# Keys and queries of the first two batches in a row ahead of the loop, and loads in another order, in a cross-attention and expert layer

## The chip, the cores and the metric

One core of one Trainium2 chip runs the whole layer. The metric is the device time of one execution in microseconds; lower is better. TensorE (PE) multiplies, VectorE (DVE), ScalarE (ACT) and GpSimd (POOL) do the elementwise work, and SyncE (SP) issues most of the DMA transfers. Each engine runs its own instructions strictly in the order in which they are written, and waits on semaphores for the others.

## The reference

Eight batches; x is 112 x 256 for each, the context 375 x 256, and attention has 16 heads of 16.

```python
q = split_heads(layernorm(x) @ Wq + bq); k = split_heads(ctx @ Wk + bk); v = split_heads(ctx @ Wv + bv)
scores = where(mask, -1e15, q @ k.T / sqrt(16))
x = x + tanh(g_xattn) * (softmax(scores) @ v @ Wo + bo)
h = layernorm(x)                      # then, for each batch, the three likeliest of 8 zones:
w = top3(softmax(tanh(mean(h) @ W1 + b1) @ W2 + b2)), normalised
x = x + tanh(g_ffn) * (h + sum_e w_e * gelu(h @ Wa[e]) @ Wb[e])
```

## The kernel before

The program has an attention stage, which is a software pipeline over the batches, and then an expert stage of 24 units (8 batches, 3 zones each). Its instructions are written out by hand for each engine.

**The pipeline.** The loop `for b in range(-2, B)` on every engine has a body for each b from -2 to 7, and each body four slots. Body b works on several batches at once: it turns batch b's scores into exponentials and sums (`st_tile`, `exp_tile`, `pv`), makes the row maxima of batch n = b + 1 (`s1` on TensorE, `row_max` on VectorE), the values of n (`V0`, `V1`), the keys and queries of batch m = b + 2 (`CX0`, `CX1`, `XT`, `K0`, `K1`, `Q`), and finishes batch o = b - 1. A step for a batch that isn't there is left out, so body -2 holds only the keys and queries of batch 0, and body -1 those of batch 1 together with row maxima and values of batch 0. The first exponential of the program is `exp_tile(0, 0, 0)`, at the head of body 0 on ScalarE.

**Keys and queries.** Context and normalised x are transposed (L1057, L1083) and copied to SBUF, K and Q are projected (L1066, L1092), ScalarE rounds them to float16 (`k_hi` L645, `q_hi` L637) and VectorE makes the remainder (`k_lo` L811, `q_lo` L819). SyncE writes both to a scratch in HBM (`write_k` L316, `write_q` L310) and, when the write has landed, reads them back in another layout (`read_k` L339, four issues for each half of the heads; `read_q` L327, two). `s1` (L1016) of a batch waits for both.

**The scratch buffers.** `k_hl`, `q_hl`, `ctx_s`, `xa`, `mask_s` and `tT` exist once. A batch's K and Q therefore wait until those of the batch before have been written, and a load into them until the batch before has been read.

**The expert weights.** While the attention runs, the weights of all 8 zones stream in through a ring (`stage`) in 64 parts, two in a slot, from slot 2 of body -1 on. One load of 512 KB brings two parts (`load_parts`, L359 and L362, on SyncE, two slots ahead of use). GpSimd scales a part (`scale_part`, L459), ScalarE rounds it (`w_hi`, L655), GpSimd makes the remainder (`lo_part`, L464). GpSimd's order in a slot is: scale the two parts of the next slot, then the norm or the bias step of this slot, then the remainders of this slot's two parts. In slot 3 of body b the norm is `norm1(b + 3)` (L469, L470). ScalarE's order at the end of a body is `v_copy` (L605), `w_hi` of the slot's two parts, `normed` (L586), which waits for that norm. `tanh_gates` (L611, L615) comes after it in body -2.

**SyncE's order in a body** is: `read_k` and `read_q` of the second half of n, `move_max(b, 1)`, parts, the loads of context and x of batch m + 1, the mask of m, parts, the writes of m, `move_max(n, 0)` (L348; `st_tile` of a batch waits for it), parts, the reads of the first half of m, parts.

**PSUM.** The small steps share three banks in turn (`MISC_BANKS`); `Spare` lists their order, and TensorE waits in `use` until the bank's last user is done.

Of the kernel before, what the change touches and what calls it, by code (L numbers as in the profile page):

```python
# [14 lines left out]
B, SQ, D, SK = 8, 112, 256, 375  # L15
# [45 lines left out]

def slot_uses(b, slot):

    n, m, o = b + 1, b + 2, b - 1
    every = (
        (("MX1", b), ("CX0", m), ("CX1", m), ("XT", m), ("OT", o), ("K0", m)),
        (("K1", m), ("Q", m), ("X2T", b - 2)),
        (("MX0", n), ("V0", n), ("ON", o)),
        (("V1", n), ("OP", o)),
    )  # L70
    more = {(B - 2, 3): ("H", 0), (B - 1, 0): ("L", 0), (B - 1, 2): ("W", 0), (-1, 3): ("BO", 0)}.get((b, slot))
    return [u for u in every[slot] if there(u[1])] + ([more] if more else [])


TAIL = {0: ("OT", B - 1), 1: ("X2T", B - 2), 2: ("ON", B - 1), 3: ("OP", B - 1), 5: ("X2T", B - 1), 7: ("H", 1), 8: ("L", 1), 11: ("W", 1)}
# [12 lines left out]
class Spare:  # L88


    def __init__(self):
        names, banks = [], []
        for b in range(-2, B):
            for slot in range(4):
                for name in slot_uses(b, slot):
                    banks.append(MISC_BANKS[len(names) % len(MISC_BANKS)])
                    names.append(name)
        for i, name in enumerate(TAIL.values()):
            names.append(name)
            banks.append(TAIL_BANKS[i % len(TAIL_BANKS)])  # L100
        self.at = {name: i for i, name in enumerate(names)}
        self.names, self.banks = names, banks
# [38 lines left out]
def flamingo_layer(nc, x, ctx, mask, g_xattn, g_ffn, Wq, bq, Wk, bk, Wv, bv, Wo, bo,  # L141
                   W1, b1, W2, b2, Wa, Wb, out):
    with ExitStack() as stack:
# [124 lines left out]
        def view_w(ap):  # L268
            return ap.rearrange("(t p) n -> p t n", p=128)
# [17 lines left out]
        def _(sp):  # L287
# [111 lines left out]
            load_ctx(0)  # L399
            sp.dma_start(wqkvo[:, 2, :, :], view_w(Wv)).then_inc(s["wv_loaded"], 16)  # L400
            for b in range(-2, B):
                n, m, o = b + 1, b + 2, b - 1
                read_k(n, 1)
                read_q(n, 1)
                move_max(b, 1)
                load_parts(b, 0)
                load_xr(o)
                load_ctx(m + 1)
                load_x(m + 1)
                load_mask(m)  # L410
                load_parts(b, 1)
                write_k(m, 0)
                write_k(m, 1)
                write_q(m)
                move_max(n, 0)
                load_parts(b, 2)
                if b == B - 1:
                    store_index(0)
                    sp.wait_ge(s["xt_done"], B)
                    load_r(0)  # L420
                    sp.wait_ge(s["misc_full"], spare.full(("V1", B - 1)))
                    load_x2(0)
                    load_x2(1)

                read_k(m, 0)
                read_q(m, 0)
                load_parts(b, 3)
                store_r(b - 2)
                store_x2(b - 2)
# [21 lines left out]
        def _(pool):  # L451
# [46 lines left out]
            pool.wait_ge(s["zeroed"], 5)  # L498
# [3 lines left out]
            g.dma_start(bo_r[:, :], bass.AP(bo.tensor, 0, [[0, 128], [1, D]])).then_inc(s["const_loaded"], 16)  # L502
            g.dma_start(w1_s[:, :, :], W1.rearrange("(t p) n -> p t n", p=128)).then_inc(s["const_loaded"], 16)
            g.dma_start(w2_s[:, :], W2).then_inc(s["const_loaded"], 16)
            g.dma_start(b1_c[:, :], b1.rearrange("(p o) -> p o", o=1), allow_slow_non_contiguous=True).then_inc(s["const_loaded"], 16)
            g.dma_start(b2_r[:, :], bass.AP(b2.tensor, 0, [[0, B], [1, NZ]])).then_inc(s["const_loaded"], 16)
            for b in range(-2, B):
                for slot in range(4):
# [9 lines left out]
                    for k in ks:  # L518
                        lo_part(k)
            norm2(B - 2)  # L520
# [4 lines left out]
        def _(act):  # L525
            a = nc.scalar
            a.dma_start(wq_in, view_w(Wq)).then_inc(s["wq_loaded"], 16)
            a.dma_start(wqkvo[:, 1, :, :], view_w(Wk)).then_inc(s["wk_loaded"], 16)
            a.dma_start(bk_c[:, :], bk.rearrange("(t p) -> p t", p=128), allow_slow_non_contiguous=True).then_inc(s["bk_loaded"], 16)
            for t in range(DT):  # L530
                a.dma_start(bq_c[:, t:t + 1], bass.AP(bq.tensor, t * 128, [[1, HD], [HD, PAIRS], [1, 1]]), allow_slow_non_contiguous=True).then_inc(s["bq_loaded"], 16)
            a.dma_start(bv_c[:, :], bv.rearrange("(t p) -> p t", p=128), allow_slow_non_contiguous=True).then_inc(s["bv_loaded"], 16)
            a.dma_start(gates[:, 0:1], bass.AP(g_xattn.tensor, 0, [[0, 128], [1, 1]])).then_inc(s["g_loaded"], 16)
            a.dma_start(gates[:, 1:2], bass.AP(g_ffn.tensor, 0, [[0, 128], [1, 1]])).then_inc(s["g_loaded"], 16)
            a.dma_start(wqkvo[:, 3, :, :], view_w(Wo)).then_inc(s["wo_loaded"], 16)
# [38 lines left out]
            def mask_bias(b):  # L574
                if there(b):
# [3 lines left out]
                    if b == 0:  # L579
                        act.wait_ge(s["zeroed"], 5)  # L580
# [88 lines left out]
            normed(0)  # L669
            act.wait_ge(s["wq_loaded"], 16)  # L670
            a.activation(wq_p[:, :, :, :], wq_in.rearrange("p k (t j i) -> p (k t) i j", t=DT, i=HD), ACT.Copy, scale=HD ** -0.5).then_inc(s["wq_scaled"], 1)
            for b in range(-2, B):
                n, m, o = b + 1, b + 2, b - 1
# [7 lines left out]
                if b == -2:  # L681
                    act.wait_ge(s["bq_loaded"], 32)
                    a.activation(bq_c[:, :], bq_c[:, :], ACT.Copy, scale=HD ** -0.5).then_inc(s["wq_scaled"], 1)
                    act.wait_ge(s["wq_scaled"], 2)
                    act.wait_ge(s["bk_loaded"], 16)
# [32 lines left out]
                normed(m + 1)  # L718
                if b == -2:
                    tanh_gates()  # L720
# [36 lines left out]
        def _(dve):  # L757
# [139 lines left out]
            v.memset(qbd[:].rearrange("p a e j f -> p (a e j f)"), 0.0).then_inc(s["zeroed"], 1)  # L897
            v.memset(vp[:].rearrange("p a c h i -> p (a c h i)"), 1.0).then_inc(s["zeroed"], 1)
            v.memset(bank[:, O_BANK, :], 0.0).then_inc(s["zeroed"], 1)
            ln1_stats(0)  # L900
            v.memset(maskb[96:KQ, :, :], 1.0).then_inc(s["zeroed"], 1)
            v.memset(pT[96:CK + 1, :, :], 1.0).then_inc(s["zeroed"], 1)
            dve.wait_ge(s["zeroed"], 5)
            for b in range(-2, B):
                n, m, o = b + 1, b + 2, b - 1
# [8 lines left out]
                if b == -2:  # L914
                    dve.wait_ge(s["wq_scaled"], 2)
                    dve.wait_ge(s["bk_loaded"], 16)
# [12 lines left out]
                ln1_stats(m + 1)  # L929
# [12 lines left out]
                if b == -1:  # L942
# [52 lines left out]
        def _(pe):  # L995
# [41 lines left out]
            def pv(b, g):  # L1037

                if there(b):
                    pe.wait_ge(s["act_exp"], tile(b, g, 2) + 1)  # L1040
                    if g == 0:
                        pe.wait_ge(s["v_done"], 2 * b + 2)
                        need(pe, s["act_o"], b)
# [137 lines left out]
            pe.wait_ge(s["zeroed"], 3)  # L1181
            for b in range(-2, B):
# [102 lines left out]
```

## Time and profile before

| | |
|---|---|
| time, median of 3 runs (lowest to highest) | 330.56 us (330.47 to 331.02) |
| the profiled execution: its own time / its span | 328.42 us / 326.3 us |
| mean granted TensorE clock | 0.984 of full |
| busy: PE, DVE, ACT, POOL | 289.3, 203.2, 195.5, 134.3 us |
| DMA | 40.51 MB, mean 124 GB/s |

The span is the time from the first to the last instruction of the profiled execution, and times inside it count from its start. Its own time is 2.1 us longer than the span. Sums are made against 328.42 us and then set against the median. "Landing" is the moment at which a transfer's semaphore is complete.

### The profile page before, as it was taken

What the parts mean: (1) busy time and instruction counts of PE and PEld (TensorE: products, weight loads), DVE (VectorE), ACT (ScalarE), POOL (GpSimd) and SP (SyncE); (2) the same over time, 40 slices, a digit from 0 to 9 for tenths busy, and PEclk for the clock granted to TensorE, in tenths of its full rate; (3) what the DMA queues carried; (4) which work ended last, traced back from release to release, by engine and by line L of the source; (5) the groups of instructions that cost most, each with busy time, mean ns of one, the idle gap of its engine ahead of it and who ended that gap; (6) DMA issues with size and microseconds to landing.
All of it is one profiled execution on the core that took longest, in us unless ns stands there. A gap on an engine that the chain in (4) does not pass through costs nothing.

```text
span 326.3 us, 9360 instructions
## 1 busy us (share of the span) xinstructions
PE 289.3 (89%) x3348; PEld 242.0 (74%) x3348; DVE 203.2 (62%) x617; ACT 195.5 (60%) x406; POOL 134.3 (41%) x185
## 2 busy tenths in 40 slices
PE   1619679899989999999989867999999999999996
PEld 1406457676766766767666646999999999999996
DVE  7417838576787777877687545656564745636542
ACT  2413466877878778777787876635454753543531
POOL 3401576867778689687788871000000000000000
PEclk9978979999999999999999999999999999999999
DMA  7458776787677977868664512101110110101000
GB/s 163 123 152 234 177 226 161 214 250 182 196 206 176 274 211 191 255 182 242 180 191 145 147 44 58 33 27 33 41 33 2 44 31 17 44 2 44 2 16 14
DMA packets 39324, 40.51 MB, mean 124 GB/s; under 512 B 10249, under 2 KB 35137, under 8 KB 39281
## 3 DMA queue, kind: packets, MB, share of 16 engines
q1 hardware_dynamic: 37168, 38.94, 42.7%
q10 hardware_dynamic: 1936, 0.79, 1.0%
q8 instruction: 28, 0.46, 0.6%
q0 software_dynamic: 176, 0.20, 0.3%
q14 instruction: 16, 0.12, 0.1%
HBM read 33.09 MB, written 6.74 MB: 122 GB/s over the span
## 4 chain that ended last, share of the span: by engine, by line
PE 64%; DMA 9%; ACT 7%; DVE 5%; issue 5%; SPq 5%; POOL 2%; ACTq 0%; DVEq 0%
PE bank L1240 18%; PE bank L1221 16%; PE bank L1066 6%; PE bank L1075 4%; PE bank L1016 4%; DMA qbd<-q_scr 4%; PE bank L1028 4%; PE bank L1032 3%; PE bank L1048 3%; ACT pT L545 2%; DMA stage<-in_L_ffn_Wa 2%; PE bank L1057 2%; SPq L339 2%; PE bank L1132 2%; ACT wa L655 2%
## 5 line engine op out<-in xcount | busy, mean ns | idle before, releaser
L769 DVE CUSTOM_DVE_ANT_0 bank<-bank,maskb 112x375 f32<-112x375 f32 x128 | 67.9, 571 | 39.8 <-PE bank L1016 39.7
L1240 PE MATMUL bank<-wb,stage 128*112 x576 | 66.8, 273 | 0.0
L1240 PEld LDWEIGHTS bank<-wb,stage 128*112 128x112 f16 x576 | 62.2, 130 | 0.2
L1221 PE MATMUL bank<-ctxT,wqkvo 128*128 128x112 f16 x960 | 59.4, 213 | 2.0 <-DVE qbd L895 1.3
L1221 PEld LDWEIGHTS bank<-ctxT,wqkvo 128*128 128x128 f16 x960 | 57.5, 98 | 2.9 <-issue 2.2
L732 ACT ACTIVATE kst<-bank 128x448 f32<-128x448 f32 x48 | 25.6, 534 | 55.4 <-PE bank L1221 55.3
L545 ACT ACTIVATE pT<-bank 125x448 f32<-125x448 f32 x96 | 48.9, 539 | 9.0 <-PE bank L1032 8.3
L894 DVE COPY wqkvo<-wa 128x3072 f16 x24 | 23.2, 969 | 48.5 <-PE bank L1221 47.5
L459 POOL TENSOR_SCALAR stage<-stage 128x512 f32<-128x512 f32 x64 | 38.5, 618 | 26.5 <-DMA stage<-in_L_ffn_Wa 21.7
L1016 PE MATMUL bank<-kst,qbd 128*112 128x375 f16 x128 | 33.8, 338 | 15.2 <-DMA qbd<-q_scr 11.8
L464 POOL TENSOR_TENSOR wb<-stage,wb 128x512 f16<-128x512 f32 x32 | 37.5, 1191 | 14.0 <-ACT wb L655 14.0
L1028 PE MATMUL bank<-rq,maskb 115*128 115x448 bf16 (+1 forms) x96 | 35.5, 370 | 7.5 <-ACT pT L545 7.1
L1221 PE MATMUL bank<-ctxT,qbd 128*128 128x112 f16 x192 | 40.9, 213 | 0.0
L464 POOL TENSOR_TENSOR wa<-stage,wa 128x512 f16<-128x512 f32 x32 | 36.4, 1159 | 10.0 <-ACT wa L655 10.0
L1032 PE MATMUL bank<-qbd,kst 128*128 128x224 f16 (+1 forms) x192 | 34.4, 260 | 0.0
L958 DVE SCALAR_TENSOR_TENSOR stage<-kst,wbc,stage 128x448 f16<-128x448 f32 x48 | 30.9, 680 | 3.9 <-ACT stage L734 3.8
L734 ACT ACTIVATE stage<-kst,wbc 128x448 f16<-128x448 f32 x48 | 32.1, 669 | 1.6
L1032 PEld LDWEIGHTS bank<-qbd,kst 128*128 128x128 f16 (+1 forms) x192 | 21.6, 113 | 11.7 <-issue 1.3
L1016 PEld LDWEIGHTS bank<-kst,qbd 128*112 128x112 f16 x128 | 15.0, 132 | 19.9 <-DMA qbd<-q_scr 12.8
L1048 PE MATMUL bank<-pT,vp 125*17 125x112 f32 (+1 forms) x768 | 24.7, 261 | 0.0
L469 POOL TENSOR_TENSOR rstd<-ve,half 112x1 f32<-112x1 f32 x16 | 8.8, 551 | 37.0 <-DVE ve L791 37.0
L1028 PEld LDWEIGHTS bank<-rq,maskb 115*128 115x128 bf16 (+1 forms) x96 | 10.7, 111 | 14.9 <-ACT pT L545 12.7
(123 smaller groups left out, 423.6 us busy)
## 6 DMA issues: line engine op xcount, KB each, us to landing
stage<-in_L_ffn_Wa SPq DMA_DIRECT2D x16, 512.0 KB, 4.3
stage<-in_L_ffn_Wb SPq DMA_DIRECT2D x16, 512.0 KB, 4.4
kst<-k_scr SPq DMA_DIRECT2D x64, 93.8 KB, 3.7
k_scr<-wb SPq DMA_DIRECT2D x16, 187.5 KB
ctx_s<-in_ctx SPq DMA_DIRECT2D x8, 336.0 KB
qbd<-q_scr SPq DMA_DIRECT2D x32, 56.0 KB, 3.1
xa<-in_x SPq DMA_DIRECT2D x8, 112.0 KB, 4.4
q_scr<-wb SPq DMA_DIRECT2D x16, 56.0 KB, 3.2
```

The costliest lines, as they stand in the source:

```text
L459: g.tensor_scalar(st, st, WSCALE, 1.0, ALU.mult, ALU.mult).then_inc(s["scaled"], 1)
L464: g.tensor_tensor(part_dst(k, 1), stage[:, k % RING, :], part_dst(k, 0), ALU.subtract).then_inc(s["lo_done"], 1)
L545: a.activation(pT[0:CK, t % PRING, :], bank[0:CK, ST_BANKS[t % len(ST_BANKS)], 0:QUAD], ACT.Exp).then_inc(s["act_exp"], 1)
L734: a.activation(hT[:, u % 2, cols], h_w[:, cols], ACT.Copy, scale=wbc[:, u:u + 1]).then_inc(s["hthi_done"], 1)
L769: v.tensor_tensor_reduce(out=bank[0:SQ, e, 0:SK], in0=bank[0:SQ, e, 0:SK], in1=maskb[0:SQ, b % 2, 0:SK], scale=-1.0, scalar=FLOOR, op0=ALU ...
L958: v.scalar_tensor_tensor(out=hT[:, u % 2, (2 + hf) * QUAD:(3 + hf) * QUAD], in0=h_w[:, cols], scalar=wbc[:, u:u + 1], in1=hT[:, u % 2, col ...
L1016: T.matmul(bank[0:SQ, e, 0:SK], qbd[:, b % 2, e, p, :], kst[:, b % 2, p * SK:(p + 1) * SK], start=True, stop=True).then_inc(s["pe_s1"], 1)
L1028: T.matmul(o[0:w, :].rearrange("k (j q) -> k j q", j=4), maskb[0:KQ, b % 2, c * CK:c * CK + w], rq[0:KQ, g // 2, :, g % 2, :], start=True, ...
L1032: ins = T.matmul(o[0:w, i * 2 * SQ:(i + 1) * 2 * SQ].rearrange("k (e q) -> k e q", e=2), kst[:, b % 2, p * SK + c * CK:p * SK + c * CK + w ...
L1048: ins = T.matmul(bank[32 * j:32 * j + VC, O_BANK, g * SQ:(g + 1) * SQ], vp[0:k, b % 2, c, h, :], pT[0:k, tile(b, g, c) % PRING, j * SQ:(j ...
L1221: ins = T.matmul(o, first(ws, t, f), x2b[:, b % 2, (xs * DT + t) * SQ:(xs * DT + t + 1) * SQ], start=(t == 0 and xs == 0 and ws == 0), sto ...
L1240: ins = T.matmul(o, hT[:, u % 2, hs * FT * SQ + f * SQ:hs * FT * SQ + (f + 1) * SQ], wb[:, bass.ds(e * (4 * CHUNK) + ws * (2 * CHUNK) + f ...
```

## The change

The keys and queries of batches 0 and 1 are made in a row ahead of the loop (`AHEAD`), and the loop starts with body -1. `made(b)` gives b + 2 from body 0 on and nothing in body -1, which now holds only the row maxima and the values of batch 0. The loads change places: Wk goes before Wq on ScalarE's queue; bk, bq, Wv, Wo, bv and the two gates go to SyncE's queue, the last four into body -1; GpSimd's five loads of constants go to the end of body -1. `tanh_gates` goes to the end of body -1, and the constant term of the output bias (`BO`, L1102) to body 0. The memsets of VectorE are spread between its first steps, and TensorE no longer waits for three of them.

```diff
+def made(b):
+    return b + 2 if b >= 0 else B
-    more = {..., (-1, 3): ("BO", 0)}.get((b, slot))
+    more = {..., (0, 3): ("BO", 0)}.get((b, slot))
+AHEAD = (("CX0", 0), ("CX1", 0), ("XT", 0), ("K0", 0), ("K1", 0), ("Q", 0),
+         ("CX0", 1), ("CX1", 1), ("K0", 1), ("K1", 1), ("XT", 1), ("Q", 1))
@@ SyncE
             load_x(0)
             load_ctx(0)
+            sp.dma_start(bk_c ...)
+            for t in range(DT): sp.dma_start(bq_c ...)
+            load_mask(0)
+            load_ctx(1)
+            load_x(1)
+            write_k(0, 0)
+            write_k(0, 1)
+            write_q(0)
+            for h in range(2):
+                read_k(0, h)
+                read_q(0, h)
             sp.dma_start(wqkvo[:, 2, :, :], view_w(Wv))
-            for b in range(-2, B):
-                n, m, o = b + 1, b + 2, b - 1
-                read_k(n, 1)
-                read_q(n, 1)
+            load_mask(1)
+            write_k(1, 0)
+            write_k(1, 1)
+            write_q(1)
+            for h in range(2):
+                read_k(1, h)
+                read_q(1, h)
+            for b in range(-1, B):
+                n, m, o = b + 1, made(b), b - 1
+                if n > 1:
+                    read_k(n, 1)
+                    read_q(n, 1)
                 move_max(b, 1)
                 load_parts(b, 0)
                 load_xr(o)
-                load_ctx(m + 1)
-                load_x(m + 1)
+                load_ctx(b + 3)
+                load_x(b + 3)
                 load_mask(m)
+                if b == -1: Wo, bv and the two gates are loaded here
                 load_parts(b, 1)
@@ GpSimd
+            norm1(1)
-            pool.wait_ge(s["zeroed"], 5)
+            pool.wait_ge(s["zeroed"], 4)
...
-            g.dma_start(bo_r ...), w1_s, w2_s, b1_c, b2_r
-            for b in range(-2, B):
+            for b in range(-1, B):
...
                     for k in ks:
                         lo_part(k)
+                    if (b, slot) == (-1, 3): the five loads of bo_r, w1_s, w2_s, b1_c, b2_r
@@ ScalarE
+            a.dma_start(wqkvo[:, 1, :, :], view_w(Wk))
             a.dma_start(wq_in, view_w(Wq))
-            the loads of Wk, bk_c, bq_c, bv_c, gates, Wo
...
             normed(0)
+            cx_copy(0)
+            xt_copy(0)
             (Wq and bq scaled)
+            k_hi(0, 0); k_hi(0, 1); q_hi(0)
+            cx_copy(1); mask_bias(0); normed(1)
+            k_hi(1, 0); k_hi(1, 1); xt_copy(1); q_hi(1); mask_bias(1)
-            for b in range(-2, B):
+            for b in range(-1, B):
...
-                normed(m + 1)
-                if b == -2:
+                normed(b + 3)
+                if b == -1:
                     tanh_gates()
@@ VectorE
             v.memset(qbd)
-            v.memset(vp); v.memset(bank)
             ln1_stats(0)
+            v.memset(bank); v.memset(maskb)
+            cx_copy(0); k_lo(0, 0); k_lo(0, 1); q_lo(0)
+            ln1_stats(1)
+            cx_copy(1)
+            v.memset(vp)
+            k_lo(1, 0); k_lo(1, 1)
             v.memset(pT)
+            q_lo(1)
-            for b in range(-2, B):
+            for b in range(-1, B):
...
-                ln1_stats(m + 1)
+                ln1_stats(b + 3)
@@ TensorE
-            pe.wait_ge(s["zeroed"], 3)
-            for b in range(-2, B):
+            for name in AHEAD:
+                put(name)
+            for b in range(-1, B):
```

## Rows read from the trace of the kernel before

**Rows 1.** The profile page, part 4: the chain that ended last, by engine.

```profile
PE 64%; DMA 9%; ACT 7%; DVE 5%; issue 5%; SPq 5%; POOL 2%; ACTq 0%; DVEq 0%
```

**Rows 2.** Stretches: length, busy us (instructions) by engine, granted clock, DMA share, GB/s.

```profile
23.60:42.40 18.80, 13.90 (x61) 9.41 (x61) 13.45 (x52) 6.91 (x16) 6.91 (x11) 0.92 0.73 198
42.40:62.96 20.56, 18.99 (x165) 13.83 (x165) 13.17 (x50) 14.56 (x33) 13.77 (x17) 0.92 0.69 196
62.96:83.10 20.14, 19.34 (x199) 14.60 (x200) 13.77 (x53) 15.57 (x36) 15.14 (x20) 1.00 0.76 213
```

**Rows 3.** Timeline, start: start, length, engine, line, what, [idle before <-releaser].

```profile
6.80 1.48 PE L1057 MATMUL bank<-ident,ctx_s 125*128 125x125 f32 x6 [6.80 <-DVE maskb L901]
...
7.21 1.93 DVE L902 MEMSET pT<- 30x2240 f32 x1 [0.42 <-issue]
...
9.98 4.25 PE L1066 MATMUL bank<-ctxT,wqkvo 128*128 128x375 f32 x8 [1.32 <-DVE ctxT L805]
...
12.94 0.57 ACT L645 ACTIVATE wb<-bank,bk_c 128x375 f16<-128x375 f32 x1 [3.55 <-PE bank L1066]
...
14.87 0.61 DVE L811 SCALAR_TENSOR_TENSOR wb<-bank,bk_c,wb 128x375 f16<-128x375 f32 x1 [0.59 <-ACT wb L645]
```

**Rows 4.** Timeline: the issues of SyncE's queue around its first reads.

```profile
14.30 1.80 SPq L316 DMA_DIRECT2D k_scr<-wb  x2
...
18.34 2.23 SPq L339 DMA_DIRECT2D kst<-k_scr  x4
...
21.93 1.97 SPq L339 DMA_DIRECT2D kst<-k_scr  x4
...
23.94 1.16 SPq L327 DMA_DIRECT2D qbd<-q_scr  x2
...
25.14 0.59 SPq L359 DMA_DIRECT2D stage<-in_L_ffn_Wa  x1
...
26.37 0.83 SPq L299 DMA_DIRECT2D ctx_s<-in_ctx  x2
...
28.10 0.43 SPq L359 DMA_DIRECT2D stage<-in_L_ffn_Wa  x1
```

**Rows 5.** Timeline: first and last of four issues on ScalarE's queue.

```profile
3.59 0.61 ACTq L532 DMA_DIRECT2D bv_c<-in_L_xattn_bv  x1
...
5.22 0.46 ACTq L535 DMA_DIRECT2D wqkvo<-in_L_xattn_Wo  x1
```

**Rows 6.** Writes of k_scr, whole run: issue to landing.

```profile
DMA to landing us min/median/max: 1.9/3.7/4.2
```

**Rows 7.** Loads of stage, whole run: issue to landing.

```profile
DMA to landing us min/median/max: 3.6/4.4/6.2
```

**Rows 8.** Timeline: GpSimd and ScalarE before the first exponential.

```profile
18.95 0.72 ACT L615 ACTIVATE wqkvo<-wqkvo,tgate 128x512 f32<-128x512 f32 x1
...
30.05 1.20 POOL L459 TENSOR_SCALAR stage<-stage 128x512 f32<-128x512 f32 x2 [11.86 <-DMA stage<-in_L_ffn_Wa]
...
37.81 2.27 POOL L464 TENSOR_TENSOR wa<-stage,wa 128x512 f16<-128x512 f32 x2 [3.60 <-ACT wa L655]
...
41.22 0.54 POOL L469 TENSOR_TENSOR rstd<-ve,half 112x1 f32<-112x1 f32 x1
...
42.07 0.60 ACT L586 ACTIVATE xa<-xa,nmr,rstd 112x256 f32<-112x256 f32 x1 [1.43 <-POOL nmr L470]
...
42.57 0.52 ACT L545 ACTIVATE pT<-bank 125x448 f32<-125x448 f32 x1
```

**Rows 9.** Timeline: TensorE at the start of body 0.

```profile
42.45 0.53 PE L1016 MATMUL bank<-kst,qbd 128*112 128x375 f16 x2 [2.11 <-DMA qbd<-q_scr]
...
44.64 0.58 PE L1028 MATMUL bank<-rq,maskb 115*125 115x448 bf16 x1
```

**Rows 10.** Timeline: last of five issues by GpSimd.

```profile
12.43 0.56 POOL L506 DMA_DIRECT2D b_r<-in_L_ffn_b  x1
```

## The prediction on record

> **What bounds the kernel now.** I read the chain that ended last first, because it says which engines the end hangs on [rows 1]. TensorE holds 64% of it; DMA, SyncE's queue and ScalarE hold another 21%. Next I cut the span at the moments at which TensorE opens a body [rows 2]. Body -1 (23.6 to 42.4) has TensorE busy 13.90 of 18.8 us, body 0 has 18.99 of 20.56, body 1 has 19.34 of 20.14. From body 0 on the attention stage is TensorE's, with almost nothing idle. A delay ahead of body 0 therefore reaches the end, and so does a gain. What counts is one moment: when body 0 can really run. I call it by `exp_tile(0, 0, 0)`, which starts at 42.57 [rows 8]. TensorE's third scores tile needs that exponential.
>
> Before 42.57 two chains arrive nearly together, and that is the point of this profile. One is the round trip of batch 1's keys and queries: TensorE waits 2.11 us for them until 42.45 [rows 9]. The other is the expert weights on GpSimd and ScalarE: remainders of parts 0 and 1 from 37.81, scaling of the next two, the norm of batch 2 at 41.22, `normed(2)` at 42.07, then the exponential [rows 8]. ScalarE and GpSimd take their work in written order, so this second chain holds the exponential as firmly as the first. The change shortens the first chain. I ask what it does to the second.
>
> **The start.** Before, VectorE's copy of the context waited behind a memset that began at 7.21 and took 1.93; K began at 9.98, its first half reached ScalarE at 12.94, and the last remainder of K ended at 14.87 + 0.61 [rows 3]. The memset goes behind the copy. The transposes, from 6.80 for 1.48, end at 8.28; a copy and the hand-over take some 0.8, so K starts at about 9.1: a gain of 0.8 to 1.1 (the context may land a little earlier, as Wv is not behind it). The eight records of K took 4.25 us, the first half of them 2.96 and the second 1.3: the first half ran at half pace. With a shorter pause of TensorE ahead of K more of it could run at the full pace, up to 1.3 more. I take a gain of 1.5 in all, with 0.8 and 2.4 as ends. The shorter memset order, the order of Wk and Wq, and TensorE's dropped wait have no price of their own beyond this: the copies they stood before are in it. The Trainium skill (TensorE: Matmul & The Clock Gate, "What's actually happening") says that the half pace ends after sustained activity; by that the gain here would be 2.4 and the total 0.9 us lower. No row before shows TensorE working through from the transposes, so I don't rest on it.
>
> **SyncE's queue, the step that decides.** Before, it ended batch 0's reads at 23.94 + 1.16 = 25.10, and issued the first load of parts at 25.14, context and x of batch 2 from 26.37, the second load of parts at 28.10; batch 1's writes and reads came only after those [rows 4]. In the change all of batch 1's round trip stands before the first load of parts:
> - reads of batch 0 end at 25.10 - 1.5 = 23.6;
> - Wv and mask 1, two issues like those of parts and context, 0.45 each: 24.5;
> - two writes of K, 0.65 each, the second issued at 25.15, and two of Q at 0.55: 26.9;
> - the second write of K lands 3.7 later [rows 6], at 28.85. SyncE waits for it with `read_k` half issued. The remaining two issues take it to 29.8, `read_q` 1.25 to 31.05, the second halves 2.0 and 1.2 [rows 4] to 34.25;
> - the first load of parts is issued at 34.25 instead of 25.14, and until 34.85;
> - two issues of context and one of x: 26.37 to 28.10 held four issues with the mask [rows 4], so 1.3: 36.15;
> - Wo, bv and two gates, which took 3.59 to 5.68 on ScalarE's queue [rows 5], 2.1: 38.25;
> - the second load of parts is issued at 38.25 instead of 28.10.
>
> The Trainium skill (DMA: Bandwidth & Descriptors, "Issuing engines are not separate DMA queues") says that a second issuing engine saves only issue time. The rows agree that this time is what counts: the four issues moved cost 2.1 us of SyncE.
>
> **From the second load to the exponential.** It lands 4.8 after its issue (the first took 4.9 to its use [rows 4, 8]; all loads 3.6 to 6.2 [rows 7]): 43.05. GpSimd then does, in its written order, two scalings 1.20, the remainders of parts 0 and 1 2.27, two scalings 1.20, and the norm 0.81 (41.22 to 42.03, by the start of what it released) [rows 8]: 48.55. The remainders can't go ahead of the scaling that waits. ScalarE does `normed(2)` 0.6 and then the moved `tanh_gates`, 0.72 and a tanh of 0.2 [rows 8]: 50.1. The exponential starts at about 50.1 instead of 42.57, 7.5 us later.
>
> **What of it reaches TensorE.** Before, TensorE's third tile began at 44.64 [rows 9], 2.07 after the exponential's start, since the late queries had also held `s1(1, 0)`. In the change `s1(1, 0)`, the second tile and the context's transposes are done while it waits, and the third tile can follow 0.6 after: 1.45 comes back. VectorE has its own wait: x of batch 2 is issued at 35.8 and lands about 40, `ln1_stats(2)` stands ahead of the last four row maxima of batch 0, and those end near 44. TensorE's V1, first tiles and transposes then end near 48.3, under cover of the 50.1; without that cover it would cost 1 to 2 us. What is queued behind ScalarE's wait is everything of body 0. `BO` moves into body 0, which TensorE fills: four passes, at most the 1.3 of half a K [rows 3], against 1.6 us idle in that body [rows 2]. I take 0.3, ends 0 and 0.9.
>
> GpSimd's five loads of constants, at 0.6 each about 3.1 (the last took 0.56 [rows 10]), now stand between remainders 2, 3 and the scaling of parts 6, 7. ScalarE wants those parts only after batch 2's queries, several microseconds on. That hides them; the load of parts 10, with `write_k(2, 0)` behind it on SyncE, goes 1 to 2 us late, but `write_k(2, 1)` is later still and sets the read. Without cover they cost up to 3.1. Batch 1's second reads leave body 0 (3.1 us of SyncE), which had nothing waiting on them.
>
> **The sum.** 7.5 - 1.45 + 0.3 = 6.4 us on 328.42, so 334.8 by the profiled execution, which stands 2.14 under the median of the runs. Against 330.56 the forecast is 337.0. For the low end: a start gain of 2.4 (-0.9), reads that never wait for a write (-1.25), parts that land in 3.6 (-1.2): 333.6, or 333.3 without `BO`. For the high end: start gain 0.8 (+0.7), writes at 4.2 (+0.5), parts at 6.2 (+1.4), `BO` at 0.9 (+0.6): 340.2.
>
> **The rivals.**
> - *Faster, because the second chain isn't the one that ends last.* The row ahead overlaps batch 1's projections with batch 0's round trip; batch 1's operands land near 34 instead of 42.4. For it speaks the 2.11 us wait [rows 9]. Then body 0 would open with the move of the maxima at about 41.5, and with the 1.45 the time would be about 328.5. It decides only if the second load of parts is issued before about 31.9 (38.25 less 6.4), and twelve read issues of 6 us stand before it. The Trainium skill (DMA: Bandwidth & Descriptors, "Rules for kernel authors") advises to issue early and wait late, which this change does for the keys and undoes for the parts. 6%.
> - *The delay is won back.* The chain holds 9% DMA and 5% SyncE [rows 1], part of it accidents of phase in later bodies, such as a load of parts that took 6.2 [rows 7]. If one or two don't recur, 3 us come back: 333.9. Against it: bodies 0 and 1 are nearly full [rows 2]. 13%.
> - *A second hold.* GpSimd's constants lose their cover, and parts and writes in body 0 go late by 3.1: 340.1, more with a slow landing. 12%.
> - *Nothing moves*, all gains and holds cancelling: 330.6. 3%.
>
> **Numbers.** The forecast has 66%, its own range 334 to 340. The range to hold 8 in 10 takes in the low and most of the high end: 333.3 to 340.2. Within 0.2% is what a measurement of this kernel can't tell from no change. Slower 91%, same 3%, faster 6%.
>
> **What would show it.** K from about 9 instead of 9.98; the loads of parts at about 34 and 38; GpSimd idle for them and `norm1(2)` near 48; ScalarE waiting for it ahead of an exponential near 50; TensorE idle some ten microseconds within batch 0's row maxima, and body 0's stretch no shorter. The prediction is wrong if the loads of parts are issued before 32, if SyncE finds batch 1's writes landed and its issues much shorter, or if bodies 1 to 6 become shorter than before.

## The result, and the profile after

The changed kernel takes 340.22 us, median of 4 runs (339.82 to 345.49), against 330.79 us for the kernel before in the same runs; the ratio is 1.0272, with a 95% interval of 1.0202 to 1.0342. It is 9.4 us slower. Medians are of all runs; a ratio leaves out single runs that took over 1.5% longer than the fastest of their kernel, so it need not be the quotient of the two medians. The forecast was slower by 6.4, at 337.0, within 333.3 to 340.2. The direction and the chain were right; the size was short by a third, and the time lies on the upper edge of the range, just outside the 334 to 340 that the forecast itself was given.

The profiled execution took 339.82 us, with a span of 337.6 against 326.3. That is 11.3 us more, not 9.4: the kernel before scatters from 327.9 to 334.0 over the 23 runs beside the last experiments, and its profiled execution (328.42) was one of its quick ones. The sum was made on the profiled execution. There the upper end of the range is 338.1 (340.2 less 2.14), and 339.82 is 1.8 above it. That the median still touches the range is luck of this scatter.

The chain that ended last now has less TensorE and more DMA, SyncE and GpSimd than in [rows 1]:

```profile
PE 59%; DMA 13%; SPq 8%; ACT 6%; POOL 6%; issue 5%; DVE 2%; ACTq 0%; DVEq 0%
```

The stretches of the changed kernel, in the columns of [rows 2]: the row maxima of batch 0 until body 0 is ready to start, the wait until TensorE's third scores tile, and the rest of body 0.

```profile
23.10:47.10 24.00, 11.46 (x30) 6.14 (x31) 12.48 (x46) 3.06 (x7) 1.21 (x2) 0.59 0.67 181
47.10:54.80 7.70, 2.94 (x19) 1.72 (x17) 1.99 (x8) 3.47 (x8) 7.27 (x10) 0.93 0.30 102
54.80:73.90 19.10, 18.30 (x156) 13.14 (x157) 11.93 (x46) 13.73 (x31) 15.49 (x22) 0.91 0.67 177
```

TensorE is busy half of the first stretch and 2.94 of 7.70 us of the second, in which GpSimd is busy 7.27: GpSimd is the holder, TensorE the held. In body 0 TensorE is full, as it was.

The start, timeline, against [rows 3]:

```profile
6.56 1.48 PE L1107 MATMUL bank<-ident,ctx_s 125*128 125x125 f32 x6 [6.56 <-DMA ctx_s<-in_ctx]
...
8.89 5.28 PE L1116 MATMUL bank<-ctxT,wqkvo 128*128 128x375 f32 x8 [0.47 <-DVE ctxT L845]
...
14.81 0.61 DVE L851 SCALAR_TENSOR_TENSOR wb<-bank,bk_c,wb 128x375 f16<-128x375 f32 x1 [1.63 <-ACT wb L673]
```

K starts 1.09 us sooner, as forecast (0.8 to 1.1). But all its eight records now ran at half pace, 5.28 us against 4.25, and the last remainder ends at 15.42 against 15.48: nothing is gained.

SyncE's queue, timeline, against [rows 4, 5]:

```profile
23.58 1.15 SPq L335 DMA_DIRECT2D qbd<-q_scr  x2
...
25.92 1.28 SPq L324 DMA_DIRECT2D k_scr<-wb  x2
...
27.25 1.97 SPq L318 DMA_DIRECT2D q_scr<-wb  x2
...
30.00 2.46 SPq L347 DMA_DIRECT2D kst<-k_scr  x4
...
35.76 1.15 SPq L335 DMA_DIRECT2D qbd<-q_scr  x2
...
36.96 0.59 SPq L367 DMA_DIRECT2D stage<-in_L_ffn_Wa  x1
...
38.95 0.43 SPq L440 DMA_DIRECT2D wqkvo<-in_L_xattn_Wo  x1
...
40.91 0.43 SPq L367 DMA_DIRECT2D stage<-in_L_ffn_Wa  x1
```

The two loads of parts go out at 36.96 and 40.91; before, 25.14 and 28.10.

GpSimd, ScalarE, VectorE and TensorE ahead of the first exponential, timeline, against [rows 8, 9, 10]:

```profile
41.61 1.21 POOL L492 TENSOR_SCALAR stage<-stage 128x512 f32<-128x512 f32 x2 [21.84 <-DMA stage<-in_L_ffn_Wa]
...
43.34 0.43 DVE L828 BATCH_NORM_STATS2 stat<-xa 112x6 f32<-112x256 f32 x1 [10.41 <-DMA xa<-in_x]
...
44.94 1.07 PE L1064 MATMUL bank<-kst,qbd 128*112 128x375 f16 x2 [9.47 <-DVE peaks L809]
...
47.45 1.20 POOL L492 TENSOR_SCALAR stage<-stage 128x512 f32<-128x512 f32 x2 [4.63 <-DMA stage<-in_L_ffn_Wa]
...
48.61 2.27 POOL L497 TENSOR_TENSOR wa<-stage,wa 128x512 f16<-128x512 f32 x2
...
52.01 0.55 POOL L502 TENSOR_TENSOR rstd<-ve,half 112x1 f32<-112x1 f32 x1
...
52.86 0.60 ACT L614 ACTIVATE xa<-xa,nmr,rstd 112x256 f32<-112x256 f32 x1 [3.55 <-POOL nmr L503]
...
54.21 0.96 ACT L573 ACTIVATE pT<-bank 125x448 f32<-125x448 f32 x2
...
54.79 0.53 PE L1076 MATMUL bank<-rq,maskb 115*125 115x448 bf16 x1 [4.75 <-ACT pT L573]
...
54.98 0.81 POOL L550 DMA_DIRECT2D bo_r<-in_L_xattn_bo  x1
```

This is the chain as it was forecast, step for step: GpSimd waits for the second load (4.63), scales, makes remainders, scales, norms; ScalarE waits 3.55 for the norm; TensorE waits 4.75 for the exponential. GpSimd's loads of constants (54.98) come right behind. The longest wait of TensorE is another one, its 9.47 us in batch 0's row maxima, behind VectorE's 10.41 us for x of batch 2. Whether that one costs anything is the first question to the experiments. The first exponential came at 54.21 (forecast 50.1), TensorE's third tile at 54.79.

### The profile page after: what moved, and what is told of

The parts are those of the page before. It is cut to its first block, busy times and chain, and to the rows that moved or that the text cites. A ratio compares the mean times of both kernels' runs of the same rounds, so it can differ in the third digit from the quotient of the medians.

```text
span 337.6 us, 9361 instructions
## 1 busy us (share of the span) xinstructions
PE 295.1 (87%) x3348; PEld 242.9 (72%) x3348; DVE 203.0 (60%) x617; ACT 195.7 (58%) x406; POOL 134.1 (40%) x185
## 3 DMA queue, kind: packets, MB, share of 16 engines
q1 hardware_dynamic: 38560, 39.21, 42.5%
## 4 chain that ended last, share of the span: by engine, by line
PE 59%; DMA 13%; SPq 8%; ACT 6%; POOL 6%; issue 5%; DVE 2%; ACTq 0%; DVEq 0%
PE bank L1291 17%; PE bank L1272 16%; PE bank L1116 6%; DMA stage<-in_L_ffn_Wa 3%; PE bank L1125 3%; PE bank L1076 3%; DMA stage<-in_L_ffn_Wb 3%; PE bank L1064 3%; SPq L347 3%; DMA k_scr<-wb 3%; PE bank L1080 2%; PE bank L1098 2%; POOL stage L492 2%; SPq L335 2%; POOL wa L497 2%
## 5 line engine op out<-in xcount | busy, mean ns | idle before, releaser
L1064 PE MATMUL bank<-kst,qbd 128*112 128x375 f16 x128 | 35.4, 351 | 13.6 <-DVE peaks L809 12.1
L497 POOL TENSOR_TENSOR wb<-stage,wb 128x512 f16<-128x512 f32 x32 | 37.6, 1195 | 11.5 <-ACT wb L683 11.5
```

What stands on the lines that cost most here:

```text
L497: g.tensor_tensor(part_dst(k, 1), stage[:, k % RING, :], part_dst(k, 0), ALU.subtract).then_inc(s["lo_done"], 1)
L1064: T.matmul(bank[0:SQ, e, 0:SK], qbd[:, b % 2, e, p, :], kst[:, b % 2, p * SK:(p + 1) * SK], start=True, stop=True).then_inc(s["pe_s1"], 1)
```

## The experiments

Twelve kernels. Each row below is read from its profiled execution: the first exponential, TensorE's third scores tile, and the first residual step of VectorE (end of body 1), which shows what has come through to the steady part of the loop. The last column is the median of its runs, the others are single executions, which scatter by some us in their later parts; the kernel before had 330.75, 331.03 and 331.04 beside the three groups (1 to 4, 5 to 8, 9 to 12).

| | first exponential | third tile | first residual | time |
|---|---|---|---|---|
| before | 42.57 | 44.64 | 82.88 | 330.8 |
| changed | 54.21 | 54.79 | 93.69 | 340.22 |
| 1 two loads of parts first | 49.84 | 50.42 | 90.03 | 336.28 |
| 2 x of batch 2 first | 54.16 | 54.74 | 93.43 | 340.20 |
| 3 three loads and x first | 46.64 | 49.46 | 87.25 | 332.29 |
| 4 before, parts late | 50.67 | 51.25 | 89.84 | 338.90 |
| 5 gates back | 49.82 | 50.40 | 92.09 | 340.16 |
| 6 constants back | 53.09 | 53.67 | 93.41 | 340.93 |
| 7 TensorE kept at work | 52.72 | 53.30 | 92.77 | 340.59 |
| 8 all moved | 44.47 | 46.36 | 83.80 | 331.61 |
| 9 gates and constants back | 50.68 | 51.26 | 88.56 | 333.53 |
| 10 all moved, reordered | 39.97 | 45.06 | 83.22 | 330.54 |
| 11 norm earlier | 50.28 | 50.86 | 94.51 | 341.57 |
| 12 before, TensorE kept at work | 45.99 | 46.57 | 83.81 | 328.55 |

**1. The first two loads of parts ahead of batch 1's reads.**

```diff
             write_q(1)
+            load_parts(-1, 0)
+            load_parts(-1, 1)
             for h in range(2):
                 read_k(1, h)
                 read_q(1, h)
```

(Here and in 2, 3, 8 and 10 the calls in the loop for what is moved are skipped in body -1.)

> The changed kernel, with the first two loads of parts issued ahead of batch 1's reads. Theory (the late loads of parts hold GpSimd, and its norm of batch 2 holds the first exponential): the second load lands near 35 instead of 47.4, the next hold is the third load, still behind everything (issued near 42, landed near 46.5), so the norm comes near 48 and the first exponential near 50 instead of 54.2; time about 4 us below the changed kernel, 336. Rival (x of batch 2, for which VectorE and TensorE wait some 10 us, is what costs): it stays late, so no gain, 340.

336.28 us, ratio to before 1.0174 (1.0127 to 1.0221); first exponential at 49.84. The third load was used at 46.48 and the norm came at 47.64, both within 0.4 of the theory; only the second load came 1.2 later than expected (36.17). x of batch 2 stayed late (42.57), so the rival is out.

**2. x of batch 2 alone ahead of batch 1's reads.**

```diff
             write_q(1)
+            load_x(2)
             for h in range(2):
```

> The changed kernel, with x of batch 2 alone issued ahead of batch 1's reads. Theory: TensorE's pause of 9.5 us in batch 0's row maxima goes, the first exponential stays near 54, the time stays at 340 within 0.5. Rival (x of batch 2 costs): the time falls by 5 us or more, to 335 or less.

340.20 us. The timeline of this kernel, VectorE's statistics, TensorE's first scores tile, and the exponential with the third tile:

```profile
32.67 0.43 DVE L830 BATCH_NORM_STATS2 stat<-xa 112x6 f32<-112x256 f32 x1 [0.25 <-DMA xa<-in_x]
...
46.48 0.56 PE L1078 MATMUL bank<-rq,maskb 115*128 115x448 bf16 x1 [9.33 <-DMA rq<-ms]
...
54.16 0.96 ACT L575 ACTIVATE pT<-bank 125x448 f32<-125x448 f32 x2
54.74 0.63 PE L1078 MATMUL bank<-rq,maskb 115*125 115x448 bf16 x1 [4.24 <-ACT pT L575]
```

VectorE's wait is gone, x was used at 32.67 instead of 43.34, and the exponential did not move by 0.1 us. TensorE's pause did not go, as the theory had it: the row maxima are done sooner, and TensorE then stands 9.33 us before its first scores tile for the move of the maxima, which SyncE issues at 40.56 behind the first two loads of parts, context 2 and the gates. That tile comes at 46.48, 1.0 sooner than in the changed kernel, and still 7.7 before the exponential. So late x of batch 2 cost nothing, because another chain ended later. The move of the maxima is a third chain, with no price as long as GpSimd's is the last.

**3. Three loads of parts and x of batch 2 ahead of batch 1's reads.**

```diff
             write_q(1)
+            load_parts(-1, 0)
+            load_parts(-1, 1)
+            load_parts(-1, 2)
+            load_x(2)
             for h in range(2):
```

> The changed kernel, with the first three loads of parts and x of batch 2 all ahead of batch 1's reads. Theory: the GpSimd chain is done near 41; the move of the maxima (landed near 44) and the gates' loads (landed near 44) hold next, the first exponential comes near 45.3; time about 8.5 us below the changed kernel, 331.5, near the kernel before. Rival (VectorE's wait alone costs): as the run with x alone. Rival (the row of keys and queries itself costs, whatever the loads do): stays above 336.

332.29 us, ratio 1.0036 (1.0003 to 1.0069). First exponential at 46.64, 1.3 later than expected. Of the 9.4 us, 7.9 come back with the row of keys and queries left exactly as it is. So the row is not what costs; its place in front of the loads is. What holds the exponential now is the third chain: TensorE's first tile waits for the move of the maxima until 45.64, and ScalarE's tanh for the gates until 45.78. In the kernel before that tile came at 39.79.

**4. The kernel before, with only its first three loads of parts behind the first half of batch 1's reads.**

```diff
-                load_parts(b, 0)
+                if b != -1:
+                    load_parts(b, 0)
...
                 read_q(m, 0)
+                if b == -1:
+                    for i in range(3):
+                        load_parts(b, i)
```

(The calls for slots 1 and 2 are guarded in the same way.)

> The kernel before, with nothing of the row: only its first three loads of parts are issued after the first half of batch 1's reads. Theory: the loads go out near 39 instead of 25 to 35, the norm of batch 2 comes near 50 and the first exponential near 51 instead of 42.6; TensorE gets 1.5 back; time 7 us above the kernel before, 337.5. Rival (the row is what costs): within 1 us of the kernel before, since its keys and queries come as before.

338.90 us, ratio 1.0272 (1.0209 to 1.0334). This is the opposite test: nothing of the row, only the late loads, and the kernel before becomes slower by 8.15 us, where the changed one is slower by 9.4. Its timeline, SyncE, GpSimd, ScalarE:

```profile
39.07 1.06 SPq L359 DMA_DIRECT2D stage<-in_L_ffn_Wa  x2
...
49.32 0.54 POOL L475 TENSOR_TENSOR rstd<-ve,half 112x1 f32<-112x1 f32 x1
...
50.16 0.60 ACT L592 ACTIVATE xa<-xa,nmr,rstd 112x256 f32<-112x256 f32 x1 [3.00 <-POOL nmr L476]
50.67 0.96 ACT L551 ACTIVATE pT<-bank 125x448 f32<-125x448 f32 x2
```

**5. Wo, bv and the gates back on ScalarE's queue, the tanh ahead of the loop.**

```diff
             a.dma_start(wq_in, view_w(Wq))
+            a.dma_start(wqkvo[:, 3, :, :], view_w(Wo)).then_inc(s["wo_loaded"], 16)
...
             mask_bias(1)
+            tanh_gates()
```

(With it the loads of bv and the two gates; the four loads on SyncE and the later tanh are taken out.)

> The changed kernel, with Wo, bv and the two gates back on ScalarE's queue at the start, and the tanh of the gates ahead of the loop. Theory: SyncE issues the second load of parts 2 us sooner and ScalarE has 0.8 us less between the norm and the first exponential: 2.8 us below the changed kernel, 337.4. Rival (those issues are hidden): no difference.

340.16 us, no difference in time, although the first exponential came 4.4 us sooner. The gain was there at the third tile (50.40), mostly gone at the first residual (92.09 against 93.69), and wholly at the last one of the attention stage (209.18 against 209.04).

**6. GpSimd's five loads of constants back ahead of its loop.**

```diff
+            g.dma_start(bo_r[:, :], bass.AP(bo.tensor, 0, [[0, 128], [1, D]])).then_inc(s["const_loaded"], 16)
...
             for b in range(-1, B):
```

(With it the four other loads; the five at the end of body -1 are taken out.)

> The changed kernel, with GpSimd's five loads of constants back ahead of its loop. Theory (they are covered in body 0): within 0.5 us of the changed kernel. Rival (a second hold): 1 to 3 us below it.

340.93 us, 0.7 above the changed kernel and so within the scatter of its runs (338.96 to 341.92): covered, as the theory says.

**7. TensorE kept at work until the first context is there.**

```diff
             pe.wait_ge(s["ident_ready"], 1)
+            for i in range(11):
+                T.matmul(bank[:, ST_BANKS[0], 0:128], ident[:, :], ident[:, :], start=True, stop=True)
             for name in AHEAD:
```

> The changed kernel, with eleven extra products of the identity on TensorE (their result is not used) while it waits for the first context, 1.7 to 6.4 us. In the changed kernel all eight passes of batch 0's K ran at half pace, 5.28 us. Theory A (TensorE must have worked without a long pause before it gets its full pace): K takes about 2.7 us, batch 0's round trip ends 2 us sooner, everything behind it as well: 338. Theory B (the pace comes with time from the start, whatever TensorE does): K stays at 5.3 us and the time at 340.

340.59 us. Its timeline, TensorE at the start:

```profile
1.68 5.00 PE L1232 MATMUL bank<-ident 128*128 128x128 f32 x22 [1.68 <-POOL ident L521]
...
8.24 2.76 PE L1116 MATMUL bank<-ctxT,wqkvo 128*128 128x375 f32 x8 [0.66 <-DVE ctxT L845]
```

K in 2.76 us instead of 5.28, and the second load of parts issued at 39.38 instead of 40.91: theory A on the pace. The first exponential followed by 1.5, the first residual by 0.9, and the median not at all. So the pace was as theory A has it, and the time was as theory B has it.

**8. All of these moves together** (experiments 3, 5 and 6, and context 2 with the move of the maxima between the halves of batch 1's reads).

```diff
             write_q(1)
+            load_parts(-1, 0)
+            load_parts(-1, 1)
+            load_parts(-1, 2)
+            load_x(2)
             for h in range(2):
                 read_k(1, h)
                 read_q(1, h)
+                if h == 0:
+                    load_ctx(2)
+                    move_max(0, 0)
```

> The changed kernel's row, with the first three loads of parts and x of batch 2 ahead of batch 1's reads, context 2 and the first move of the maxima between their halves, the gates, bv and Wo back on ScalarE's queue with an early tanh, and GpSimd's constants ahead of its loop. Theory: nothing is left in front of the norm of batch 2 but two landed loads; the first exponential comes near 41.5, TensorE's third tile near 42.3 instead of 44.6: 328.5, about 2 us below the kernel before. Rival (the row costs in itself, by half-pace work of TensorE or by crowding of the transfers): 331 or more.

331.61 us, ratio 0.9997 (0.9948 to 1.0046): the same as the kernel before, not 2 us better. The first exponential came at 44.47, 3 us later than expected. x of batch 2 was issued at 30.15, right behind three loads of 512 KB, and used at 38.16; the move of the maxima, 5 KB issued at 35.36, was used at 42.86. Both engines were waiting for them when they came (5.77 and 0.33 us). These two small transfers, behind large ones on one queue, took 7 to 8 us. The rival's "crowding" is what the trace shows.

**9. Experiments 5 and 6 together.**

> The changed kernel with both parts moved back at once: Wo, bv, the gates and their tanh, and GpSimd's five loads of constants. Alone, the first brought the first exponential forward by 4.4 us and the second by 1.1, and neither brought the time below the changed kernel's. Theory (second hold: with the gates back, GpSimd's five issues, 3.1 us, stand before the remainders on which the load of parts 10 and the write of K behind it wait): the first exponential near 49, the write of batch 2's K waits for nothing but VectorE; 336.5, 3.5 us below the changed kernel. Rival (the gain is lost in later bodies, to TensorE's half pace): 339 to 341.

333.53 us, ratio 1.0108 (1.0051 to 1.0165). Two edits that did nothing alone save 6.7 us together (340.22 less 333.53), more than the 3.5 expected. Against experiment 5 the first residual is 3.5 sooner and the last one of the attention stage 6.2 (202.99 against 209.18), so nearly half of the gain comes in later bodies, where it was not followed. How the first part comes about is seen with experiment 11.

**11. Only GpSimd's norm of batch 2 moved, from slot 3 to slot 2 of body -1.**

```diff
                 for slot in range(4):
                     ks = parts_at(b, slot)
+                    if (b, slot) == (-1, 2):
+                        norm1(b + 3)
                     for k in parts_at(b + (slot + 1) // 4, (slot + 1) % 4):
                         scale_part(k)
...
-                    if slot == 3:
+                    if slot == 3 and b > -1:
                         norm1(b + 3)
```

> The changed kernel with one thing moved, no load and no transfer: GpSimd's norm of batch 2 is done in slot 2 ahead of the scaling of parts 2 and 3, not in slot 3 behind four scalings and two remainders. Theory (GpSimd's written order holds the first exponential): ScalarE's wait moves from the norm to the second load of parts (47.4); the first exponential comes at 50.7 instead of 54.2; time 3 us below the changed kernel, 337. Rival (the exponential is held by something else): no difference.

The exponential at 50.28 for 50.7 expected: no load moved, and the move of the norm in GpSimd's written order alone gave 3.9 us. That shows the first hold. But the time is 341.57, no better than the changed kernel's. The timeline of experiment 11, GpSimd and SyncE, then TensorE at batch 2's first row maxima:

```profile
47.17 1.20 POOL L492 TENSOR_SCALAR stage<-stage 128x512 f32<-128x512 f32 x2 [2.35 <-DMA stage<-in_L_ffn_Wa]
...
51.74 2.28 POOL L497 TENSOR_TENSOR wa<-stage,wa 128x512 f16<-128x512 f32 x2
...
53.95 0.81 POOL L552 DMA_DIRECT2D bo_r<-in_L_xattn_bo  x1
...
58.31 2.29 POOL L497 TENSOR_TENSOR wb<-stage,wb 128x512 f16<-128x512 f32 x2
...
60.63 0.35 SPq L367 DMA_DIRECT2D stage<-in_L_ffn_Wa  x1
...
61.03 1.30 SPq L324 DMA_DIRECT2D k_scr<-wb  x2
...
73.22 0.88 PE L1066 MATMUL bank<-kst,qbd 128*112 128x375 f16 x2 [4.71 <-DMA qbd<-q_scr]
```

The same place in experiment 9:

```profile
53.58 2.28 POOL L492 TENSOR_TENSOR wb<-stage,wb 128x512 f16<-128x512 f32 x2
...
55.88 0.36 SPq L367 DMA_DIRECT2D stage<-in_L_ffn_Wa  x1
56.28 3.45 SPq L324 DMA_DIRECT2D k_scr<-wb  x2
```

The second hold is the forecast's rival of that name, in the place that it gave: GpSimd's constants. GpSimd's five issues (53.95 to 57.13) stand before the remainders of parts 4 and 5; SyncE waits for those to load parts 10 and 11 (60.63), and behind that load, in its order, stands the write of batch 2's K (61.03). When body 0 starts sooner, its K is ready sooner, but this chain moves by only 1.0 us: TensorE then waits 4.71 us, until 73.22. In the changed kernel it began this step at 73.76, so of the 3.9 us 0.5 are left. In experiment 9 the load goes at 55.88, the write is issued before its second half is ready, and TensorE has no such wait: it begins the step at 68.65. In the changed kernel the write went at 62.06, and SyncE then stood some 1.3 us for the second half (two issues of 0.65 in 2.58 us): that was all the cover the second hold had. The forecast priced the constants at up to 3.1 us; the wait is 4.71, and the medians of 5 and 9 lie 6.6 apart.

TensorE's clock adds to a hold. Windows of the changed kernel and of experiment 11 from that step on, in the columns of [rows 2]:

```profile
73.76:80.00 6.24, 6.24 (x64) 4.51 (x68) 3.50 (x15) 5.78 (x14) 5.37 (x7) 1.00 0.89 248
```

```profile
73.20:80.00 6.80, 6.78 (x56) 4.77 (x57) 2.79 (x10) 4.84 (x12) 4.32 (x6) 0.77 0.59 157
```

After its pause of 4.71 us TensorE has a mean granted clock of 0.77 there, part of the time at its lower level, and the changed kernel, which did not pause, 1.00. That is 1.6 us of full pace missing (an estimate, 0.23 of 6.8), and experiment 11 takes 1.4 us more than the changed kernel from this step to the first residual (21.29 against 19.93). So the 0.5 us that were left are gone: 94.51 instead of 93.69. The executions differ in their clock later on too, for a cause that wasn't followed. The same two kernels at the end of the attention stage:

```profile
206.00:211.00 5.00, 4.53 (x79) 3.28 (x79) 2.93 (x9) 2.06 (x4) 0.40 (x1) 1.00 0.44 127
```

```profile
206.00:211.00 5.00, 5.00 (x61) 3.16 (x59) 1.88 (x4) 1.63 (x3) 0.00 (x0) 0.66 0.43 121
```

From the sixth to the seventh residual step, around this window, the one takes 14.8 us and the other 16.5.

**10. Everything moved, in another order.**

```diff
             write_q(1)
+            load_x(2)
+            load_parts(-1, 0)
+            load_parts(-1, 1)
+            read_k(1, 0)
+            move_max(0, 0)
+            read_q(1, 0)
+            load_parts(-1, 2)
+            read_k(1, 1)
+            read_q(1, 1)
```

(With the edits of experiments 5, 6 and 7, and GpSimd's norm ahead of the scaling in slot 3.)

> The row kept, with everything off its two holds: x of batch 2 and then two loads of parts ahead of batch 1's reads, the move of the maxima and the third load of parts between their halves, the gates, bv, Wo and GpSimd's constants at the start as before, the norm of batch 2 ahead of the scaling in its slot, and eleven unused products that keep TensorE at work before the first context. Theory: K of batch 0 in 2.8 us, x of batch 2 landed near 33, the first exponential near 40, TensorE's third tile near 41 instead of 44.6: 327.3, 3.5 us below the kernel before. Rival (crowding of the transfers, or half pace in body -1, takes it back): 330 or more.

330.54 us, ratio 0.9968 (0.9926 to 1.0011). The first exponential came at 39.97, as expected, 2.6 us before that of the kernel before. But the third tile came at 45.06. Its timeline, TensorE:

```profile
38.60 0.53 PE L1074 MATMUL bank<-kst,qbd 128*112 128x375 f16 x2 [1.27 <-DMA qbd<-q_scr]
...
43.78 1.48 PE L1117 MATMUL bank<-ident,ctx_s 125*128 125x125 f32 x6 [4.07 <-DMA ctx_s<-in_ctx]
```

The context of batch 2, pushed behind everything else and issued at 37.06, is what TensorE now waits for. With the known holds removed, the next transfer in the queue becomes the hold. The time is the rival's 330 or more, not the 327.3 of the theory, and the row of keys and queries gives nothing that can be told from the kernel before. Against experiment 12, which has the same eleven products without the row, it is 2.0 us slower.

**12. The kernel before with TensorE kept at work as in 7.**

> The kernel before with the eleven unused products on TensorE while it waits for the first context. K of batch 0 took 4.25 us there, its first half at half pace. Theory: K in 2.8 us and everything behind it 1.5 us sooner: 1.5 us below the kernel before. Rival (nothing or less comes through, since later stretches at half pace fall otherwise): within 0.7 us.

328.55 us, ratio 0.9903 (0.9856 to 0.9949): the only version that beats the kernel before, by 2.5 us where 1.5 were expected. But its profiled execution (329.44) doesn't show the expected mechanism. Its timeline, and a window over K:

```profile
6.76 0.83 PE L1057 MATMUL bank<-ident,ctx_s 125*128 125x125 f32 x6
...
9.98 4.45 PE L1066 MATMUL bank<-ctxT,wqkvo 128*128 128x375 f32 x8 [1.91 <-DVE ctxT L805]
```

```profile
9.98:14.43 4.45, 4.45 (x10) 2.63 (x11) 0.61 (x1) 0.58 (x1) 3.00 (x5) 0.62 0.61 166
```

The context's transposes ran at full pace (0.83 us instead of the 1.48 of [rows 3]). Then TensorE stood idle for 1.91 us, because VectorE's copy was still behind its memset, and K ran at a granted clock of 0.62 on the mean, and began no sooner than before. The first exponential was 3.4 later than in the kernel before. The gain is measured; its cause is open.

## Why the prediction was right, and where it was short

- **Two chains near 42.5, and the second decides.** Right. Experiment 2 excludes late x of batch 2, 11 moves the exponential through GpSimd's order alone, 1 and 3 bring 3.9 and 7.9 us back through the loads alone, 4 makes most of the loss in the kernel before. But the first chain was not shortened as the rival *Faster* had it, with the move of the maxima in place at about 41.5: it landed near 46.5 in experiment 2 and near 45.6 in 3, since SyncE issues it behind context 2, the gates and parts. In 3, with the parts in time, the third tile came at 49.46, still behind the 44.64 of the kernel before.
- **The start, 1.5 us gained.** Wrong: 0.06 at the last remainder, 0.37 at the end of batch 0's reads (24.73 against 25.10). K began where the sum put it and then ran wholly at half pace, for which the range had no end. The rule of the Trainium skill that I weighed (TensorE: Matmul & The Clock Gate, "What's actually happening"), that sustained activity ends the half pace, was to make this gain 2.4. Here the shorter pause (0.47 us instead of 1.32) did not bring the full pace to any pass of K. Experiment 7, with 5.0 us of work before, had it in all of them, as the rule says.
- **SyncE's queue.** The order and count of issues were right. The reads ended at 36.91 instead of 34.25, and that is the whole 2.66 us by which the second load was late (40.91 against 38.25): 1.13 are the start, 0.87 batch 1's two writes of Q, which took 1.97 instead of 1.1, and the rest is small items ahead of the first read. (Wv was on this queue in the kernel before as well; what was new is its place, behind batch 0's reads.) The stretches after it came out as summed (3.95 from load to load, forecast 4.0).
- **The landing of the second load.** 4.8 forecast, 6.5 measured (40.91 to 47.45): 1.74 more. It had the first load, context, x and Wo in front of it in the queue. The term was mis-sized, by more than the 6.2 that the high end allowed.
- **From the load to the exponential.** 7.05 forecast, 6.76 measured.
- **The part that TensorE gets back.** 0.6 from exponential to third tile, 0.58 measured. In all the third tile is 10.15 late, forecast 6.05; the 4.1 between them are the 2.66, the 1.74 and -0.29 above.
- **`BO` and body 0.** From the third tile to the first residual 38.90 against 38.24, so 0.7 for the forecast's 0.3. `BO` was not tried by itself.
- **Cover of VectorE's wait.** Right: TensorE's work behind it ended at about 50.0 (L1107) under the 54.2, where the forecast had 48.3 under 50.1.
- **Cover of GpSimd's constants.** Right alone (experiment 6), and thin, as 5, 9 and 11 show. The rival *A second hold* named 340.1, nearly the time measured, but not for the reason: without those loads in body 0 the time stays (340.93).
- **Nothing won back later.** Right: the third tile is 10.15 late, the first residual 10.81, the last one inside the attention stage 11.5 (209.04 against 197.58).

So the mechanism was right and the size short: the start and the landing came out beyond the ends that they were given, and the writes of Q had been given none. The medians lie 9.4 apart and the profiled executions 11.4; that is the scatter of the runs, which was not in the sum, and it is what brought the median to the edge of the range.

## What to carry to other kernels

An engine that works in written order can be held by a step that belongs to another stream: before moving a long series on one queue ahead of a loop, list what the loop's first steps need from that queue, the unrelated prefetches above all. The longest wait in a profile need not cost anything; take its cause away alone and look whether the next stage moves, and what the engine waits for instead. And two edits that each do nothing can be worth several microseconds together when two holds end close to each other.

## What the runs showed of the hardware

- TensorE ran K's eight passes in 5.28 us (changed kernel), 4.25 (before) and 2.76 (experiment 7). The granted clock reads 1.00 over K in all three, so at the start of these programs the durations, not the record, tell the pace. In experiment 12, after full pace and a pause of 1.91 us, the record does show it: 0.62 over a K of 4.45 us.
- After a pause of 4.71 us the mean granted clock was 0.77 over the next 6.8 us, where the changed kernel without the pause had 1.00 (experiment 11).
- Transfers with large ones in front of them on their queue took long: 5 KB were used 7.5 us after their issue behind context and parts (experiment 8), 112 KB 8.0 us after, where the median landing of x in the kernel before was 4.4.
- Runs of one and the same kernel spread by 6 us (327.88 to 333.96). Among the kernels here the stretch from 206 to 211 ran at a granted clock of 1.00 in one and of 0.66 in another; that this is what spreads the runs of one kernel was not shown.
